# Linear attention's scores leave PSUM by one VectorE multiplication with the causal mask, not by a ScalarE copy and a GpSimd multiplication

## What is computed

```python
x = x + linear_attention(layernorm(x))          # phi(q), phi(k); phi = elu + 1
x = x + cross_attention(layernorm(x), ctx)      # softmax over 128 keys
x = x + ffn(layernorm(x))                       # 256 -> 1024 -> 1024 -> 1024 -> 256

# linear attention, causal, as cumulative sums
num = einsum('bhsd,bhsde->bhse', q, cumsum(k[..., :, None] * v[..., None, :]))
den = einsum('bhsd,bhsd->bhs',   q, cumsum(k))
out = (num / (den[..., None] + 1e-6)) @ Wo.T + bo
```

## Time and profile before

| | us |
|---|---|
| median of 3 runs | 1138.85 (1137.8 to 1141.24) |
| the profiled execution | 1139.79 |
| its span in the trace | 1137.9 |
| TensorE busy | 1090.2 (96% of the span) |
| VectorE busy | 647.2 (57%) |
| ScalarE busy | 605.7 (53%) |
| GpSimd busy | 365.5 (32%) |

### The profile page before, as it was taken

How to read it: one execution, slowest core, us unless ns; L and a number is a source line. 1 busy time by engine, 2 the same in 40 slices (tenths; PEclk the granted TensorE clock), 3 DMA queues, 4 the chain that set the end, 5 groups by cost and what they waited for, 6 DMA issues and landing times.

```text
span 1137.9 us, 25341 instructions
## 1 busy us (share of the span) xinstructions
PE 1090.2 (96%) x10114; PEld 902.2 (79%) x10114; DVE 647.2 (57%) x1452; ACT 605.7 (53%) x1037; POOL 365.5 (32%) x394
## 2 busy tenths in 40 slices
PE   4777999999999999999999999999999999999997
PEld 4665868888887888888888887888888887778786
DVE  4656755458544685556565575546855566534521
ACT  3345563736548364575646556474654746454432
POOL 3444361142604245052431426123360424400300
PEclk9899999999999999999999999999999999999999
DMA  4243545335323443235332353333532353334742
GB/s 117 66 149 106 184 148 187 98 108 193 123 89 119 142 158 134 85 113 179 112 132 94 112 196 118 109 104 113 197 111 99 115 171 117 121 108 133 242 148 76
DMA packets 62503, 148.63 MB, mean 131 GB/s; under 512 B 5936, under 2 KB 21424, under 8 KB 62384
## 3 DMA queue, kind: packets, MB, share of 16 engines
q1 hardware_dynamic: 58928, 135.44, 36.3%
q10 hardware_dynamic: 3456, 11.54, 3.2%
HBM read 130.17 MB, written 28.31 MB: 139 GB/s over the span
## 4 chain that ended last, share of the span: by engine, by line
PE 90%; DVE 4%; issue 2%; POOL 2%; ACT 2%; DMA 1%; ACTq 0%; SPq 0%; POOLq 0%; DVEq 0%
PE bank L1001 41%; PE bank L986 9%; PE bank L829 8%; PE bank L882 8%; PE bank L855 5%; PE bank L1016 5%; PE bank L839 4%; PE bank L818 2%; PE bank L941 2%; PE bank L864 2%; POOL att_l L503 1%; PE bank L875 1%; DVE mx L749 1%; PE bank L932 1%; PE bank L959 1%
## 5 line engine op out<-in xcount | busy, mean ns | idle before, releaser
L503 POOL TENSOR_TENSOR att_l<-att_l,cst 128x512 f32<-128x512 f32 x128 | 167.1, 1320 | 287.9 <-ACT att_l L577 287.3
L1001 PE MATMUL bank<-hidden_b,weight_ring 128*128 128x512 f32 x1024 | 257.6, 398 | 0.3
L1001 PE MATMUL bank<-hidden_a,weight_ring 128*128 128x512 f32 x1024 | 255.9, 398 | 0.0
L1001 PEld LDWEIGHTS bank<-hidden_a,weight_ring 128*128 128x128 f32 x1024 | 185.7, 188 | 41.4 <-issue 3.4
L1001 PEld LDWEIGHTS bank<-hidden_b,weight_ring 128*128 128x128 f32 x1024 | 184.8, 188 | 40.5 <-issue 3.7
L637 ACT ACTIVATE hidden_full<-bank,columns_sb 128x512 f32<-128x512 f32 x128 | 88.1, 689 | 193.4 <-PE bank L1001 192.4
L518 POOL TENSOR_TENSOR hidden_a<-hidden_full,hidden_a 128x512 fp32r<-128x512 f32 x64 | 83.3, 1305 | 161.0 <-ACT hidden_a L632 160.1
L986 PE MATMUL bank<-hidden_b,weight_ring 128*128 128x512 f32 x512 | 133.6, 399 | 0.9 <-DMA weight_ring<-weights_scratch 0.6
L788 DVE TENSOR_TENSOR hidden_a<-hidden_full,hidden_a 128x512 fp32r<-128x512 f32 x64 | 46.2, 721 | 117.9 <-ACT hidden_a L643 117.4
L986 PEld LDWEIGHTS bank<-hidden_b,weight_ring 128*128 128x128 f32 x512 | 91.1, 188 | 18.5 <-DMA weight_ring<-weights_scratch 1.0
L788 DVE TENSOR_TENSOR hidden_b<-hidden_full,hidden_b 128x512 fp32r<-128x512 f32 x64 | 46.4, 725 | 97.4 <-ACT hidden_b L643 97.3
(11 more groups left out here) (120 smaller groups left out, 1717.3 us busy)
## 6 DMA issues: line engine op xcount, KB each, us to landing
weight_ring<-weights_scratch SPq DMA_DIRECT2D x160, 512.0 KB, 3.4
weights_scratch<-in_h ACTq DMA_DIRECT2D x16, 512.0 KB, 4.9
xn3T_scratch<-hidden_b SPq DMA_DIRECT2D x16, 512.0 KB, 6.1
weight_ring<-weights_scratch SPq DMA_DIRECT2D x32, 256.0 KB, 2.7
weight_bits<-in_h SPq DMA_DIRECT2D x32, 256.0 KB, 3.9
x_in<-in_x SPq DMA_DIRECT2D x16, 256.0 KB, 3.5
xb<-in_x SPq DMA_DIRECT2D x16, 256.0 KB, 4.4
ctx_in<-in_ctxT SPq DMA_DIRECT2D x16, 256.0 KB, 4.1
```

The costliest lines, as they stand in the source:

```text
L503: eng.tensor_tensor(slot, slot, causal.rearrange("p (o s) -> p o s", o=1).broadcast_to([P, 4, S]), ALU.mult)\
L1001: mm = eng.matmul(pbank(step, g, n)[:, :], ring[:, slot, kk * P:(kk + 1) * P], src[:, part, kk, :], start=(kk == 0 and part == 0), stop=(k ...
```

## The change

The ScalarE copy and the GpSimd multiplication of a score tile become one VectorE instruction that reads the bank and the mask and writes the slot of `att_l`. The bank is now freed by VectorE, and `lin_sums` waits for VectorE. The nominal times of nearly all steps are new numbers, `JOIN` goes from 1.59 to 1.44, and the begin of the groups stays but for a hundredth. The core of the diff:

```diff
-    JOIN = 1.59
+    JOIN = 1.44
...
         for n in range(NU):
-            u = 0.29 + 1.09 * n
-            steady("lin_copy", n, scalar=u + 0.16, gpsimd=u - 1.05)
+            u = 0.34 + 1.09 * n
+            steady("lin_mask", n, vector=u + 0.02)
...
-                    "xn3T": ("vector", "xn3T", in_done, 1), "lin_scores": ("scalar", "lin_copy", lin_c, NU),
+                    "xn3T": ("vector", "xn3T", in_done, 1), "lin_scores": ("vector", "lin_mask", lin_a, NU),
...
-                    elif step == "lin_copy":
-                        eng.wait_ge(lin_c, NU * g + n + 1)
-                        if g == 0 and n == 0:
-                            eng.wait_ge(consts_loaded, 16)
-                        slot = att_l[:, (NU * g + n) % NL, :, :]
-                        eng.tensor_tensor(slot, slot, causal.rearrange("p (o s) -> p o s", o=1).broadcast_to([P, 4, S]), ALU.mult)\
-                           .then_inc(lin_a, 1)
...
-                    elif step == "lin_copy":
-                        eng.wait_ge(lin_s, GB * g + n // 4 + 1)
-                        wait_count(eng, summed[0], (NU * g + n - NL) // 2 + 1)
-                        eng.activation(att_l[:, (NU * g + n) % NL, :, :], pbank("lin_scores", g, n)[:, :].rearrange("p (j s) -> p j s", j=4), ACT.Copy)\
-                           .then_inc(lin_c, 1)
...
+                    elif step == "lin_mask":
+                        eng.wait_ge(lin_s, GB * g + n // 4 + 1)
+                        wait_count(eng, summed[0], (NU * g + n - NL) // 2 + 1)
+                        if g == 0 and n == 0:
+                            eng.wait_ge(consts_loaded, 16)
+                        eng.tensor_tensor(att_l[:, (NU * g + n) % NL, :, :],
+                                          pbank("lin_scores", g, n)[:, :].rearrange("p (j s) -> p j s", j=4),
+                                          causal.rearrange("p (o s) -> p o s", o=1).broadcast_to([P, 4, S]), ALU.mult).then_inc(lin_a, 1)
```

More of the change, by code:

```diff
@@ L74, in decoder_layer_program @@
                 if early:
-                    u = 2.15 + 5.4 * b + 2.64 * h
+                    u = 2.15 + 5.15 * b + 2.64 * h
                 else:
-                    u = 4.18 + 7.01 * b + 0.02 * h
-                steady("lin_sums", 2 * b + h, tensor=u + 0)
-            steady("lin_out", b, scalar=u + 1.76)
+                    u = 4.18 + 7.14 * b + 0.02 * h
+                steady("lin_sums", 2 * b + h, tensor=u - 0.32)
+            steady("lin_out", b, scalar=u + 1.21)
             u = 7.2 + 4.71 * b
[L81 to L88, removed]
+            steady("lin_turn", b, tensor=u - 0.39, vector=u + 0.5)
+            steady("o_turn", b, tensor=u + 0.93, scalar=u + 3.59, vector=u + 2.25)
+            steady("project", b, tensor=u + 3.88, vector=u + 5.03, gpsimd=u + 6.25)
+            steady("ln2", b, vector=u + 6.35)
+        steady("ln2T", tensor=17.76, scalar=17.95, vector=18.63)
+        steady("xq", tensor=21.95, scalar=22.34)
+        steady("xk", tensor=16.76, scalar=20.6)
+        steady("xv", tensor=11.7, scalar=16.21)
         for b in range(GB):
-            steady("max", b, tensor=23.11 + 2 * b)
-            steady("x_scores", b, tensor=29.31 + 3 * b)
+            steady("max", b, tensor=23.23 + 2 * b)
+            steady("x_scores", b, tensor=29.28 + 3 * b)
         for n in range(NU):
             b, u = n // 4, n % 4
-            steady("max_of", n, vector=24.21 + .72 * n)
-            w = 30.6 + 3.51 * b + 0.13 * u
-            steady("x_exp", n, scalar=w + 0.04)
+            steady("max_of", n, vector=24.37 + .72 * n)
+            w = 30.6 + 3.45 * b + 0.09 * u
+            steady("x_exp", n, scalar=w + 0.1)
         for b in range(GB):
@@ L99, in decoder_layer_program @@
                 if early:
-                    u = 31.71 + 3.07 * b + 0.45 * h
+                    u = 31.71 + 3.3 * b + 0.45 * h
                 else:
-                    u = 31.34 + 3.72 * b + 0.01 * h
-                steady("x_sums", 2 * b + h, tensor=u - 0.13)
-            steady("x_out", b, scalar=u + 1.02)
+                    u = 31.3 + 3.72 * b + 0.01 * h
+                steady("x_sums", 2 * b + h, tensor=u - 0.16)
+            steady("x_out", b, scalar=u + 0.97)
             u = 27.61 + 4.05 * b
[L106 to L109, removed]
+            steady("shift", b, vector=u - 0.83, tensor=u - 0.87, scalar=u + 0.61)
+            u = 34.4 + 6.37 * b
+            steady("x_turn", b, tensor=u - 2.05, vector=u - 0.14, gpsimd=u + 3.54)
+            steady("ln3", b, vector=u + 3.67)
     for n in range(7):
@@ L171, in decoder_layer_program @@
                 u = QUARTER * (2 * KH + 4 * (j - 7)) + .3
-            put(at, "ring", f, j, sync=u + 0.07)
+            put(at, "ring", f, j, sync=u - 4.82)
         for j in range(NCH):
```

56 lines of the change are left out of this document (28 added, 28 removed).

## The result

The kernel after takes **1130.73 us** (median of 6 runs, 1129.23 to 1132.54), the kernel before beside it 1139.93 us (6 runs, 1137.49 to 1141.24): ratio 0.9924, 95% interval 0.9912 to 0.9936, 9 us less. The forecast was 1135.0 with a range of 1130.0 to 1141.5. The direction was right, but the gain is two to three times the one worked out: the time lies 0.7 us inside the lower end of the range, and outside the case of 1133 to 1137.5 that was held most likely.

The account below looks back on a forecast made before the run. TensorE's own matmuls bound the kernel from 142 us on, so only idle time, mostly in the start, could be won. -3.3 + 1.9 - 1.5 - 2.0 + 0.8 + 0.4 = -3.7 us gave 1135.0 us, range 1130.0 to 1141.5.

Parts of the forecast that it names:

- the case of 1133 to 1137.5: Whole kernel: the forecast's own case, 1133 to 1137.5 us, given 0.50.
- group 0, to `project`: Start: masked tiles ready sooner, so `project` near 31.0 us instead of 34.33: -3.3 us, bounds -5.5 and -2.
- group 1, to `xq` at 78.64: From about 50 us: masks woven among VectorE's `max_of` delay TensorE: +1.9 us, bounds 0 and +3.5.
- group 2, to the first `gate`: Before the first `gate`: sums and `project` start earlier, `gate` near 114.2 us: -1.5 us, bounds -2.8 and -0.5.
- behind the first `gate`: From 142 us: division waits go (-2.0), new waits (+0.8), attention steps further apart (+0.4): -0.8 us.
- The instruction: VectorE's new mask multiplication, 128 times: 0.69 us each, bounds 0.68 and 0.75, adding 88 us to VectorE.
- The walk: Groups 0 to 2: step-by-step timing of masks, splits and sums, giving -3.3, +1.9 and -1.5 us.
- the new order as a cost (+0.4): TensorE's list: three more rows as attention steps stand apart more, +0.4 us, bounds 0 and 1.1.
- Gain eaten in group 1: Rival: from 50 to 66 us VectorE is the bound, +3.5 us, group 0 only -2; 1138.5 us, chance 0.22.
- The slower rival: Steady part: masks ahead of divisions use up the 0.69 us to spare; about +5 us, 1144 us, chance 0.13.
- More idle time goes: Rival: clock stays up in group 0 or more idle time goes; about -9 us, 1130 us, chance 0.15.
- The sign for the first `gate`: End of the start: first `gate` matmul near 112.8 us if right, at or behind 115.7 us if wrong.

Follow-up runs that it names:

- operation alone: Kernel before with its own order; only ScalarE's copy and GpSimd's multiplication replaced by VectorE's multiplication: 1134.9 us, ratio 0.9965.
- best version: Kernel after with all its numbers, but group 1 keeps ScalarE's copy and GpSimd's multiplication: 1128.16 us, run again 1127.76 us.

## Why the prediction was right, and where it fell short

The result is inside the range by its lower edge, and not by the sum that was worked out. The profiled difference of -9.1 us against the sum of -3.7, by its steps:

| step | predicted | after | operation alone |
|---|---|---|---|
| group 0, to `project` | -3.3 | -3.4 | -4.1 |
| group 1, to `xq` at 78.64 | +1.9 | +1.4 | +1.7 |
| 78.64 to 98.74 | none | -2.35 | -1.0 |
| group 2, to the first `gate` | -1.5 | -3.0 | -1.8 |
| behind the first `gate` | -0.8 | -1.8 | -1.7 |
| sum | -3.7 | -9.1 | -6.9 |

(The trace of the operation alone is of its fastest execution, 1132.84 us; by the medians it is worth 4.4.)

- *The instruction* was sized right: 684 ns against 0.69 us taken. The rest of VectorE's instructions wasn't: I had GpSimd's effect on two of them (`shift`, `low_bits`) and not the 39 us over all. `shift`'s first instruction is never above 205 ns now.
- *Group 0* came out as walked: `lin_sums` at 21.95 (said 22.2), `project` at 30.95 (said near 31), the window from 30 to 36 us still mostly at half clock. (The walk speaks of three splits between masks 2 and 4; the list has two there, and 25.0 us is what two give.) It lasted only because GpSimd's list was empty: with spare work there the second `project` comes 3.5 us later than in the operation alone, in part by the clock, and by the first `gate` all is gone. The prediction took the masks off GpSimd as "169 us off engines that don't bound". GpSimd's busy share was low, but short things that VectorE waits for, the bias in group 0 and rstd later, stood behind its masks, and its work made VectorE's other instructions longer. **That is the step of the mechanism that failed**: the shorter path was given the whole gain and the removed GpSimd work was priced at nothing in the start, where the runs show 0.9965 with GpSimd free and 0.9998 with it full. The figures for groups 0 and 1 came out all the same, since the walk took it for granted that nothing of GpSimd's comes late.
- *Group 1* came out near the walk: from the first scores to `x_scores` +2.6 us (said +2.8), in the operation alone +2.7, and with the old path there 0.0, 0.9 and -0.1. The 0.9 is that of the execution with a stretch at 1.2 GHz in this place, which after and the operation alone had too. So the masks among the maxima are about 1.7 of the 2.6 us; the rest is the clock, which had no term, and that the figure came out so near is in part luck.
- *78.64 to 98.74 us* had no term. Before ran at half clock from 78.4 to 81.8 and from 88.6 to 92.0 us, the kernel after did not. The best version won 0.8 and 0.4 us there, and both its executions had half clock between 73 and 85 us, as the operation alone (1.0) had; so I put 0.4 to 1.0 us down to the change and the rest, some 1.4 to 2 of the 9.1 us, to the clock: luck, since no term had it. That is an estimate; no run sets them apart. What makes the clock fall in one execution and not in another is open.
- *Group 2*: my -1.5 is near the -1.8 of the operation alone. The other 1.2 us are the new order's, and the best version has the same -3.0. **The second failure**: I priced the new order as a cost (+0.4) and left what it gives at nothing. With the operation it takes the ratio from 0.9965 to 0.9924, about half of the gain; with the old path it costs 65 us. Which of its new numbers give it was not tested.
- *Behind the first `gate`* the sum was 1 us short (-1.8 against -0.8), and its reasons were not these. Without masks on GpSimd the division waits stayed under the old order (0.87 and 0.75 us), so `low_bits` was only part of their cause; the new order took them away, to 0.3 us. The first two turns got 1.7 and 0.8 us shorter, where in the operation alone they got 0.3 shorter and 0.2 longer, so that is the new order's too; the next three stayed within 0.1 us. The sixth got 3.1 longer and what comes behind it 2.6 shorter: after's trace had a stretch at half clock from 802 to 806 us, which before's had not; that turn took 137.37 us where the best version's took 135.97.

The rivals. "Gain eaten in group 1" had the right place, but group 1 took 1.4 and not 3.5 us, and group 0 gave 3.4 and not 2. The slower rival is out by the kernel after itself: TensorE idles 3.2 us from 142 to 1040 us, and no division is waited for over 0.3 us. With twice the masks it begins to be true: its mark of over 1 us a turn was met in two turns. "More idle time goes" (1130, given 0.15) has the right time, though not for its reason: the clock in group 0 did not stay up. Its terms also add up to -10.3 and not "about -9", which is 1129. The sign for the first `gate`, 112.8, was missed by 4.4 us (108.39), on the good side.

The rule of the Trainium skill (SBUF — State Buffer, Who interferes with whom), by which VectorE and GpSimd take their shared ports as an exclusive lock, is borne out further than I used it: the mask with its PSUM input took 684 ns in the kernel after and 682 with spare work on GpSimd, while x + o, with both inputs in SBUF, has a mean of 425 ns from 142 us on in the operation alone and 889 in before.

## What to carry to other kernels

When work leaves an engine of low busy share, look in its list for the short instructions behind it that others wait for: here the shorter path alone, with GpSimd kept full, was worth nothing, and a bias addition or an rstd behind its long instructions was what others waited for. An order of the work and the operations in it are priced together, by walking the new list with the new durations: the new order with the old operations was 65 us slower than the old pair. And compare the clock rows of two traces before a difference of 1 to 2 us between them is put down to the change. Where the receiving engine has no pauses in one stretch, leave that stretch on the old path: one group of sixteen was worth 2.6 to 3.0 us by the medians, though the intervals touch.

## What the runs showed of the hardware that was not expected

- Some of VectorE's instructions with SBUF inputs lose more to GpSimd than thought. Under the old order, from 142 us on, and with nothing changed but where the masks are made (first the kernel before, then the operation alone):

```profile
L765 DVE TENSOR_TENSOR x<-x,o 128x256 f32<-128x256 f32 x28 | 24.9, 889 | 1.0
L798 DVE TENSOR_SCALAR weight_bits<-weight_bits 128x512 int32<-128x512 int32 x37 | 23.8, 644 | 1.4 <-DMA weight_bits<-in_h 1.4
```

```profile
L794 DVE TENSOR_SCALAR weight_bits<-weight_bits 128x512 int32<-128x512 int32 x37 | 17.5, 472 | 1.2 <-DMA weight_bits<-in_h 1.2
L761 DVE TENSOR_TENSOR x<-x,o 128x256 f32<-128x256 f32 x28 | 11.9, 425 | 1.0
```

- It goes the other way too: GpSimd's addition of the bias had a mean of 1574 ns in before and 1286 in after. Ten of its 16 executions in before took 1.74 us, each beside VectorE's subtraction for `hidden`, which has both inputs in SBUF; none in after took over 1.34.
- Two executions of the best version had their stretches at 1.2 GHz in different places (50.2 to 53.6 and 80.9 to 84.3 us; 22.2 to 25.6 and 73.4 to 80.2 us).
